# A two-layer graph and expert network on one core: record filling in small pieces, a last chunk 392 wide, and results added back by adding transfers

## The chip, the core and the metric

The kernel runs on one core of one Trainium2 chip. The core has five engines with queues of their own: TensorE (PE, matmuls into PSUM), VectorE (DVE), ScalarE (ACT), GpSimd (POOL) and SyncE (SP, here only a DMA queue). ScalarE and GpSimd issue DMAs too. All meet through semaphores: an instruction waits until a counter has reached a value. The metric is the device time in microseconds; lower is better. Before the change it was 1638.95 us, the median of 3 runs (1637.38 to 1642.18).

## What is computed

Inputs are 5000 rows of 128 features and a 5000 x 5000 adjacency of zeros and ones. Two layers follow each other, each a graph part and an expert part (mixture of eight experts, two per row):

```
x = x + gnn0(ln(x))  # A = adj * (y @ y.T); A / row_sum|A|; 0.9 * A @ ln(x) + 0.1 * h0
x = x + ffn0(ln(x))  # shared expert (hidden 512) + two of 8 private experts, weights from softmax
x = x + gnn1(ln(x))  # [x, adj @ x, sum_j adj[i,j] * adj[j,i]] @ weight + bias
x = x + ffn1(ln(x))  # two of 8 experts (hidden 256), erf-gelu
```

Everything is float32, the large products partly as a high and a low part of a shorter type (`F32R`, in the profile `fp32r`) that are multiplied separately and added.

## The kernel before

The 5000 rows are padded to 5120 = 10 column chunks of 512 (`CH`, `CW`) = 40 blocks of 128 (`NB`). `xres` holds the running x in SBUF, `xn` its norm. The kernel has four stages.

**First loop** (`a_iteration`, chunks k = 0 to 9, and two rounds more that drain). Chunk k has 43 steps s. In each of the first 40 steps PE makes a block `s` = y y^T, VectorE multiplies it with the adjacency block from `ring` into `m` (L1298), PE adds `xn` times `m` into the bank `agg` (L637), ScalarE takes |m| into `mabs` (L937), and PE adds groups of four `mabs` for the row sums (`d`, L681). `m` has four buffers, `mabs` eight. For some chunk pairs the outgoing adjacency is loaded too (`adj_out`); VectorE multiplies both (L1308), and PE sums the columns (`u`, L693). Beside this, at fixed steps (`A_AT`), chunk k-1 goes through the rest: division, residual, norm, router, and the scatter of its rows to DRAM by expert (`rows_scratch`, GpSimd, L1511), and chunk k-2 goes through the shared expert.

**Record filling.** Each expert's weights are gathered into one record in DRAM (`blob_scratch`), so that one DMA fetches them per tile. A record is: high and low part of the first weights, made by ScalarE (`whigh`) and VectorE (`wlow`) from `stage`, and the rest (second weights, biases), which goes from DRAM to DRAM. `store_rest` issues the rest on ScalarE's queue in step 6 of chunk 1, ten DMAs in a row. `wlow` has room for four experts, so `up_low(5)` must wait until the first half is stored (`low_written`).

**Expert tiles, layer 0** (`run_tiles(0, TILES)`): 27 tiles of 512 rows; the weighted results are scattered by GpSimd to `y_scratch` (L1520), two results per row in two halves (c = 0, 1).

**Second loop** (`z_iteration`). In pass k = 0, SyncE loads both halves of the results back chunk by chunk (`load_back`, L404) into `y_back`, VectorE adds them to `xres` (`back_add`, L1376), makes statistics, GpSimd the power -0.5 (L1497), VectorE the norm (L1041), ScalarE the high copy (L978), VectorE the low part. PE follows with the products of chunk column 0 (L768). Passes k = 1 to 9 (1 and 2 written out, 3 to 9 a hardware loop, `Fori`) split three of four adjacency blocks into high and low (ScalarE L989, VectorE L352) and multiply three times (L773 to L775). Beside this chunk k-1 goes through the graph weights, norm, router and row scatter, at the steps in `Z_AT`. `copy_aux`, `product`, `norm` (step 16), `weights` (33) and `scatter` (36) are such steps. The expert tiles of layer 1 and the output follow.

SyncE's queue is one list in order: all adjacency loads, the loads of the tiles, `load_back`, the loads of the second loop. Each engine's order is the order in which the code above is written out; nothing is reordered.

## Time and profile before

| | us |
|---|---|
| median of 3 runs (lowest, highest) | 1638.95 (1637.38, 1642.18) |
| profiled execution, its own time | 1639.02 |
| its span | 1637.2 |

| engine | busy us | share of the span |
|---|---|---|
| PE | 1397.8 | 85% |
| PEld (weight loads) | 864.9 | 53% |
| DVE | 967.8 | 59% |
| ACT | 646.0 | 39% |
| POOL | 541.9 | 33% |

The span is the time from the first to the last instruction in one profiled execution; 1.8 us of the device time lie outside it. Busy time overlaps between engines, so shares do not add up to one. The share of PE is a mean over stages: the first loop lasts to about 781 us, its drain to 830, the tiles of layer 0 to 1037, the second loop to 1461 (with its drain), the tiles of layer 1 to 1612, the rest is output. Line numbers (L637) are those of the kernel before. The letters in the rows below: `x8` is the number of instructions merged; in a timeline the bracket at the end says how long the engine had been idle and what ended it; `<-issue` is idle time that nothing in the profile explains.

### The profile page before, as it was taken

To read this page: it belongs to the slowest core of one execution; us is meant where nothing else is said; L and a number is where in the kernel's file an instruction comes from. 1 tells how busy PE (TensorE), PEld (TensorE's weight loads), DVE (VectorE), ACT (ScalarE), POOL (GpSimd) and SP (SyncE) were. 2 spreads that over 40 slices of the span, in tenths; PEclk is the share of its full clock that TensorE was granted. 3 is DMA by queue.
4 is the path that set the end of the run, shared out by engine and by line. 5 is a ranking of instruction groups with operands and counts; after the bars stand their busy time and mean duration, and the time that the engine had idled before them with its cause. 6 is when DMAs were issued, how large, how long until landed. Compare 5 with 4: busy or idle time off the path is not lost.

```text
span 1637.2 us, 22158 instructions
## 1 busy us (share of the span) xinstructions
PE 1397.8 (85%) x6742; PEld 864.9 (53%) x6742; DVE 967.8 (59%) x2697; ACT 646.0 (39%) x1067; POOL 541.9 (33%) x490
## 2 busy tenths in 40 slices
PE   5927699999999999999769999589999999838770
PEld 2413344444445454444558888346666666537660
DVE  7715475867676767676322322577777777633333
ACT  3504344434444434444224444135555555313330
POOL 1001101112020202112215555315555566537773
PEclk9968899999999999999779999799999999958995
DMA  9776788769696868785345554388888988436655
GB/s 324 266 224 209 284 303 311 284 245 326 252 339 229 331 226 322 250 309 201 148 156 189 180 192 156 114 309 297 306 296 302 311 294 312 142 91 184 183 164 195
DMA packets 105682, 399.29 MB, mean 244 GB/s; under 512 B 18800, under 2 KB 31123, under 8 KB 72819
## 3 DMA queue, kind: packets, MB, share of 16 engines
q1 hardware_dynamic: 63424, 337.25, 59.3%
q10 hardware_dynamic: 29330, 37.07, 6.8%
q0 software_dynamic: 12832, 23.81, 4.1%
q8 instruction: 47, 0.77, 0.2%
q14 instruction: 49, 0.39, 0.1%
HBM read 343.77 MB, written 59.51 MB: 246 GB/s over the span
## 4 chain that ended last, share of the span: by engine, by line
PE 56%; issue 12%; DVE 11%; POOL 8%; DMA 7%; ACTq 3%; ACT 2%; SPq 1%; DVEq 0%; POOLq 0%
PE agg L637 18%; PE s L621 6%; PE d L732 6%; PE d L681 5%; POOL y_scratch L1520 4%; POOL rows_scratch L1511 3%; PE d L577 3%; PE agg L768 2%; PE u L693 2%; DVE adj_over_wb L352 2%; PE u L717 2%; ACTq L848 2%; PE agg L773 1%; DMA rows_scratch<-xrow,idx 1%; PE u L719 1%
## 5 line engine op out<-in xcount | busy, mean ns | idle before, releaser
L637 PE MATMUL agg<-m,xn 128*128 128x512 f32 x800 | 411.1, 600 | 0.0
L1298 DVE TENSOR_TENSOR m<-s,ring 128x512 f32<-128x512 f32 x400 | 273.4, 687 | 226.6 <-PE s L621 144.9
L937 ACT ACTIVATE mabs<-m 128x512 f32<-128x512 f32 x400 | 247.6, 629 | 367.7 <-DVE m L1298 321.5
L621 PE MATMUL s<-ymov,ysta 128*128 128x512 f32 x400 | 258.8, 651 | 39.1 <-DVE m L1298 25.7
L1520 POOL DMA_INDIRECT y_scratch<-yo,ids x216 | 214.3, 992 | 168.5 <-DVE yo L1210 97.1
L1511 POOL DMA_INDIRECT rows_scratch<-xrow,idx x160 | 190.4, 1190 | 184.2 <-DVE idx L1141 98.8
L637 PEld LDWEIGHTS agg<-m,xn 128*128 128x128 f32 x800 | 153.9, 192 | 73.8 <-issue 53.0
L1497 POOL TENSOR_TENSOR rstd<-vareps,mhalf 128x4 f32<-128x4 f32 x30 | 35.0, 1167 | 455.1 <-DVE vareps L1035 455.1
L964 ACT ACTIVATE h<-u,wb 128x512 f32<-128x512 f32 x162 | 111.4, 688 | 173.0 <-PE u L719 172.5
L621 PEld LDWEIGHTS s<-ymov,ysta 128*128 128x128 f32 x400 | 76.4, 193 | 187.3 <-issue 102.7
L352 DVE TENSOR_TENSOR adj_over_wb<-ring,adj_over_wb 128x512 fp32r<-128x512 f32 x216 | 141.5, 686 | 47.4 <-ACT adj_over_wb L989 43.4
L732 PE MATMUL d<-wb,h 128*128 128x128 f32 x1296 | 164.7, 278 | 0.2 <-ACT h L964 0.2
L732 PEld LDWEIGHTS d<-wb,h 128*128 128x128 f32 x1296 | 160.1, 195 | 5.4 <-issue 0.6
L768 PE MATMUL agg<-ring,xn 128*128 128x512 f32 x260 | 131.7, 610 | 24.6 <-DVE xn L1041 24.6
L989 ACT CAST adj_over_wb<-ring 128x512 fp32r<-128x512 f32 x216 | 129.3, 620 | 54.6 <-PE agg L775 50.1
L681 PE MATMUL d<-mabs,ones 128*32 128x512 f32 x800 | 107.4, 609 | 39.1 <-ACT mabs L937 39.1
L1196 DVE TENSOR_TENSOR xnfl<-s,xnfh 128x512 fp32r<-128x512 f32 x54 | 37.2, 688 | 153.5 <-ACT xnfh L954 153.5
L773 PE MATMUL agg<-adj_over_wb,ysta 128*128 128x512 f32 x216 | 111.3, 515 | 14.5 <-DVE adj_over_wb L352 6.8
L717 PE MATMUL u<-xnfh,wb 128*128 128x512 f32 x162 | 76.1, 470 | 32.1 <-DVE xnfl L1196 27.1
L1559 POOL TENSOR_TENSOR ex<-euler,lg 128x8 f32<-128x8 f32 x40 | 74.5, 1887 | 59.9 <-DVE lg L1063 59.9
L1308 DVE CUSTOM_DVE_ANT_0 ring<-ring 128x512 f32<-128x512 f32 x132 | 89.7, 681 | 7.1 <-DMA ring<-in_adj_out 7.1
L775 PE MATMUL agg<-adj_over_wb,xnl 128*128 128x512 f32 x216 | 85.0, 394 | 0.0
(197 smaller groups left out, 1854.7 us busy)
## 6 DMA issues: line engine op xcount, KB each, us to landing
ring<-in_adj_in SPq DMA_DIRECT2D x200, 1024.0 KB, 5.8
ring<-in_adj_out SPq DMA_DIRECT2D x33, 1024.0 KB, 8.7
stage<-in_adj_out SPq DMA_DIRECT2D x22, 1024.0 KB, 8.8
wb<-blob_scratch SPq DMA_DIRECT2D x27, 834.0 KB, 4.5
rows_scratch<-yo ACTq DMA_DIRECT2D x81, 260.0 KB, 5.7
xt<-rows_scratch SPq DMA_DIRECT2D x54, 260.0 KB, 3.8
wb<-blob_scratch SPq DMA_DIRECT2D x27, 449.0 KB, 4.1
y_back<-y_scratch SPq DMA_DIRECT2D x10, 512.0 KB, 3.8
```

The lines of the kernel that those rows point to most:

```text
L352: return eng.tensor_tensor(low, raw, high.bitcast(F32), ALU.subtract)
L621: pe.matmul(sbank[s % 2][:], ysta[:, s * P:(s + 1) * P], ymov[:, k % 2, :], start=True, stop=True).then_inc(s_made, 1)
L637: pe.matmul(abank[:], xn[:, b, :], m[:, b % M_BUFS, :], start=b == 0, stop=b == NB - 1).then_inc(S["agg_blocks"], 1)
L681: last = pe.matmul(dbank[1][32 * i:32 * i + 32, :], ones[:, 0:32], mabs[:, (g * GROUPS + i) % ABS_BUFS, :], start=g == 0, stop=g == NB // ...
L732: last = pe.matmul(dbank[t % 2][:, q * D:(q + 1) * D], h[:, n % H_BUFS, q * P:(q + 1) * P], tile_part(t, "down", hb), start=hb == 0 and q ...
L768: pe.matmul(abank[:], xn[:, b, :], ring[:, l % 5, b % LB * CW:(b % LB + 1) * CW], start=b == 0, stop=b == NB - 1).then_inc(S["agg_blocks"], 1)
L773: pe.matmul(abank[:], xnh[:, b, :], hi, start=b == 0, stop=False)
L937: act.activation(mabs[:, b % ABS_BUFS, :], m[:, b % M_BUFS, :], ACT.Abs).then_inc(abs_made, 1)
L989: act.copy(adj_part(0, s), ring[:, l % 5, (s % LB) * CW:(s % LB + 1) * CW]).then_inc(adj_high, 1)
L1298: dve.tensor_tensor(m[:, s % M_BUFS, :], sbank[s % 2][:], slot_part(LOAD_AT[k, l, False][0], s % LB), ALU.mult).then_inc(m_made, 1)
L1511: pool.indirect_dma_start(out=rows_dram, out_offset=bass.IndirectOffsetOnAxis(ap=idx[:, t, c:c + 1], axis=0), in_=xrow[:, t, c, :], in_off ...
L1520: pool.indirect_dma_start(out=y_dram[layer], out_offset=bass.IndirectOffsetOnAxis(ap=ids[:, buf, q:q + 1], axis=0), in_=yo[:, buf, q, :], ...
```

## The change

It has three parts.

1. `store_rest` takes a piece number. A piece is one expert's slice (128 rows) or a row broadcast over all experts; there are 66 (`REST`), one in every fourth step from chunk 2 on. Of the low halves, VectorE makes only those of the shared expert and of experts 1 to 4 in chunk 1, the others in chunk 2, steps 4 to 7; the second low store moves from step 36 of chunk 1 to step 10 of chunk 2, the stores of layer 1 from step 24 to step 30, their splits from step 18 to step 22.
2. `width(k)` is 392 for the last chunk, else 512. In both loops loads, products, sums and splits of that chunk take 392 columns. For this the last pass of the second loop is written out, and the loop runs from 3 to 8. The semaphores `ring2_landed` are gone; `ring_landed` goes on counting.
3. `y_back`, `load_back` for layer 0 and `back_add` are gone. GpSimd issues twenty DMAs that add (`accum_op`) the two halves to `xres`, the second half of a chunk after the first has landed. The norm of pass 0 is made by ScalarE as `rstd * x + shift_n`, with `shift_n` from VectorE.

```
-                    if s == 6:
-                        act.wait_ge(b2_written, 32)
-                        act.wait_ge(small_landed, 16 * 7)
-                        store_rest(0)
-                        store_rest(1)
...
+                if agg and k > 1 and s % 4 == 0 and (k - 2) * NB // 4 + s // 4 < REST and s < NB:
+                    if k == 2 and s == 0:
+                        act.wait_ge(b2_written, 32)
+                        act.wait_ge(small_landed, 16 * 7)
+                    store_rest((k - 2) * NB // 4 + s // 4)
...
+        def store_rest(piece):
+            layer = 0 if piece < REST_OF[0] else 1
+            hid, piece = HID[layer], piece - layer * REST_OF[0]
+            e, i = divmod(piece, hid + 1)
+            if e == E:
+                row = b2_dram[1:1 + E, 0, :] if layer == 0 else b2_dram[0:E, 1, :]
+                act.dma_start(blob_dram[layer][:, :, 3 * hid * D:(3 * hid + 1) * D],
+                              row.unsqueeze(1).to_broadcast([E, P, D])).then_inc(rest_written, 16)
+            elif i == hid:
+                bias, first = ((b1, HID[0]), (b1z, 0))[layer]
+                act.dma_start(blob_dram[layer][e, :, (3 * hid + 1) * D:], bias[:, first + e * hid:first + (e + 1) * hid]).then_inc(rest_written, 16)
+            else:
+                act.dma_start(blob_dram[layer][e, :, (2 * hid + i) * D:(2 * hid + i + 1) * D],
+                              (w2p, w2_1)[layer][e, i * P:(i + 1) * P, :]).then_inc(rest_written, 16)
...
-                    if s == 36:
-                        store_low(0, 1)
...
-                        act.wait_ge(up_split, 1 + E)
+                        act.wait_ge(up_split, 1 + E // 2)
...
+                    if s == 10:
+                        store_low(0, 1)
...
-                if isinstance(k, int) and k == 1 and 24 <= s <= 24 + E:
+                if isinstance(k, int) and k == 1 and 24 <= s <= 24 + E // 2:
...
+                if isinstance(k, int) and k == 2 and 4 <= s < 4 + E // 2:
+                    up_low(1 + E // 2 + s - 4)
...
+def width(k):
+
+    return N - (CH - 1) * CW if isinstance(k, int) and k == CH - 1 else CW
...
-                    pe.matmul(abank[:], xn[:, b, :], m[:, b % M_BUFS, :], start=b == 0, stop=b == NB - 1
+                    pe.matmul(abank[:, 0:n], xn[:, b, :], m[:, b % M_BUFS, 0:n], start=b == 0, stop=b == NB - 1
...
-        with eng.Fori(3, CH) as k:
+        with eng.Fori(3, CH - 1) as k:
             iteration(k, True, True)
+        iteration(CH - 1, True, True)
...
-        for j in range(CH):
-            wait(sp, back_chain, 4 * (j - YIN_BUFS) + 2)
-            load_back(sp, y_back[:, j % YIN_BUFS], 0, j, yback_landed[j % YIN_BUFS])
...
+        def add_back(j, c):
+            pool.dma_start(xres[:, j * TB:(j + 1) * TB, :].rearrange("p t d -> p (t d)"),
+                           y_dram[0].rearrange("(c p b) d -> c p (b d)", c=2, p=P)[c, :, j * TB * D:(j + 1) * TB * D],
+                           accum_op=ALU.add).then_inc(yback_added[j % YIN_BUFS][c], 16)
+        def add_second(j):
+            pool.wait_ge(yback_added[j % YIN_BUFS][0], 16 * (j // YIN_BUFS + 1))
+            if j >= YIN_BUFS:
+                pool.wait_ge(yback_added[j % YIN_BUFS][1], 16 * (j // YIN_BUFS))
+            add_back(j, 1)
...
+        for j in range(YIN_BUFS):
+            add_back(j, 0)
+        for j in range(2):
+            add_second(j)
+            add_back(YIN_BUFS + j, 0)
...
                     power(s, back_var, back_rstd, s // TB + 1)
+                    if s // TB + 2 < CH:
+                        add_second(s // TB + 2)
+                    if s // TB + 2 + YIN_BUFS < CH:
+                        add_back(s // TB + 2 + YIN_BUFS, 0)
...
+            for b in range(c * TB, (c + 1) * TB):
+                last = act.activation(xn[:, b, :], xres[:, b, :], ACT.Identity, bias=shift_n[:, b:b + 1],
+                                      scale=rstd[:, b:b + 1])
```

ScalarE in chunk 1 of the first loop, before: after the copies of `b2rows` and four products the ten DMAs of the rest (`w2p`, `w_1` second weights, `b`, `b1z` biases, `b_scratch` rows) stand in a row.

```order
L864 DMA b_scratch<-b2rows 8x128
L937 ACTIVATE mabs<-m 128x512 x4
L848 DMA blob_scratch<-in_w2p 1024x1x128 x4
L851 DMA blob_scratch<-b 128x8x4
L854 DMA blob_scratch<-b_scratch 1024x1x128
L848 DMA blob_scratch<-in_w_1 1024x1x128 x2
L851 DMA blob_scratch<-b1z 128x8x2
L854 DMA blob_scratch<-b_scratch 1024x1x128
L822 DMA rows_scratch<-yo 128x520
```

The same place now, in which only the null rows (L840, before L822) stand between the products:

```order
L886 DMA b_scratch<-b2rows 8x128
L959 ACTIVATE mabs<-m 128x512 x4
L840 DMA rows_scratch<-yo 128x520
L959 ACTIVATE mabs<-m 128x512 x4
L840 DMA rows_scratch<-yo 128x520
```

The ten DMAs are gone from here; single ones, of 128 rows, now stand between products from chunk 2 on, as here in its steps 24 to 28:

```order
L876 DMA blob_scratch<-in_w2p 128x128
L959 ACTIVATE mabs<-m 128x512 x2
L840 DMA rows_scratch<-yo 128x520
L959 ACTIVATE mabs<-m 128x512 x2
L876 DMA blob_scratch<-in_w2p 128x128
```

GpSimd between the last result scatter of layer 0 and the second loop's router, before and now: the powers (`rstd`) of the ten chunks stood alone (the eleventh belongs to pass 1).

```order
L1520 DMA y_scratch<-yo,ids 10240x128 x108
L1497 TENSOR_TENSOR rstd<-vareps,mhalf 128x4 x11
L1559 TENSOR_TENSOR ex<-euler,lg 128x8 x4
```

```order
L1549 DMA y_scratch<-yo,ids 10240x128 x108
L1578 DMA xres<-y_scratch 128x512 x8
L1526 TENSOR_TENSOR rstd<-vareps,mhalf 128x4
L1578 DMA xres<-y_scratch 128x512 x2
L1526 TENSOR_TENSOR rstd<-vareps,mhalf 128x4
L1578 DMA xres<-y_scratch 128x512 x2
L1526 TENSOR_TENSOR rstd<-vareps,mhalf 128x4
```

Eight adding DMAs now come ahead of the first power, and two behind each of the next four. On VectorE the same stretch loses the adds and the norms and gets one small instruction a chunk; before:

```order
L1376 TENSOR_TENSOR xres<-xres,y_back 128x512 x2
L1024 BN_STATS stats<-xres 128x6 x4
L1032 BN_AGGR mv<-stats 128x2 x4
L1035 TENSOR_SCALAR vareps<-mv 128x4
L1041 TENSOR_SCALAR xn<-xres,mv,rstd 128x128 x4
L352 TENSOR_TENSOR xnl<-xn,ysta 128x512
```

and now:

```order
L1056 BN_STATS stats<-xres 128x6 x4
L1064 BN_AGGR mv<-stats 128x2 x4
L1067 TENSOR_SCALAR vareps<-mv 128x4
L1412 SCALAR_TENSOR_TENSOR shift_n<-mv,rstd 128x4
L361 TENSOR_TENSOR xnl<-xn,ysta 128x512
```

The two adds on `xres` and the four norms have left VectorE; the norms stand on ScalarE (`xn<-xres,shift_n,rstd`), ahead of its high copy.

## Rows read from the trace of the kernel before

**Rows 1.** windows of the first loop: chunk 1's stall, chunk 2, chunk 9.

```profile
core 0: us, PE busy (x) PEld busy (x) DVE busy (x) ACT busy (x) POOL busy (x), PEclk, DMA share, GB/s
77.00:128.00 51.00, 15.43 (x68) 7.29 (x67) 11.12 (x29) 5.32 (x11) 0.00 (x0) 0.70 0.74 231
190.00:270.00 80.00, 75.22 (x343) 36.24 (x342) 55.59 (x153) 34.21 (x56) 10.79 (x11) 0.98 0.87 314
...
708.00:781.00 73.00, 72.39 (x344) 35.43 (x340) 50.31 (x139) 30.21 (x51) 10.50 (x11) 1.00 0.61 221
```

**Rows 2.** waits of 78 to 190 us: us in all, times, longest.

```profile
PE d L681 <- ACT mabs L937: 36.1, 1, 36.1
...
PE s L621 <- DVE m L1298: 15.4, 3, 14.0
DVE wlow L352 <- DMA blob_scratch<-wlow: 15.1, 1, 15.1
```

**Rows 3.** timeline of ScalarE (start us, us): the `aggf` copies that open and end chunk 1.

```profile
77.15 0.59 ACT L916 COPY aggf<-agg 128x512 f32<-128x512 f32 x1 [1.22 <-PE agg L637]
...
191.94 0.59 ACT L916 COPY aggf<-agg 128x512 f32<-128x512 f32 x1 [1.22 <-PE agg L637]
```

**Rows 4.** two lines of DMA issues on ScalarE's queue, ns min/median/max.

```profile
L848 ACTq DMA_DIRECT2D blob_scratch<-in_w2p x4: 822/4411/8657, 85.5 to 100.2; - x4
...
L822 ACTq DMA_DIRECT2D rows_scratch<-yo x81: 338/338/3473, 22.0 to 769.1; - x81
```

**Rows 5.** waits of 190 to 270 us, chunk 2 of the first loop.

```profile
DVE ring L1308 <- DMA ring<-in_adj_out: 7.1, 2, 6.0
```

**Rows 6.** timeline of TensorE in chunk 9 of the first loop.

```profile
771.26 1.07 PE L681 MATMUL d<-mabs,ones 128*32 128x512 f32 x8
...
773.68 1.02 PE L637 MATMUL agg<-m,xn 128*128 128x512 f32 x2
...
774.77 1.02 PE L637 MATMUL agg<-m,xn 128*128 128x512 f32 x2
```

**Rows 7.** chain of waits in chunk 2: one group of eight column sums.

```profile
205.55 0.90 PE u L693 x8
```

**Rows 8.** groups of 708 to 781 us by shape: count, busy us, mean ns, idle before.

```profile
L1298 DVE TENSOR_TENSOR m<-s,ring 128x512 f32<-128x512 f32 x40 | 27.3, 688 | 22.0 <-PE s L621 16.5 <-issue 5.1 <-ACT mabs L937 0.3
```

**Rows 9.** timeline, start of the second loop: SyncE's queue, then PE, VectorE and GpSimd.

```profile
1039.33 27.12 SPq L404 DMA_DIRECT2D y_back<-y_scratch  x10
...
1050.67 1.22 PE L768 MATMUL agg<-ring,xn 128*128 128x512 f32 x1 [19.55 <-DVE xn L1041]
...
1058.32 1.11 DVE L1041 TENSOR_SCALAR xn<-xres,mv,rstd 128x128 f32<-128x128 f32 x4
...
1059.94 1.41 DVE L1376 TENSOR_TENSOR xres<-xres,y_back 128x512 f32<-128x512 f32 x2
...
1063.03 1.11 DVE L1041 TENSOR_SCALAR xn<-xres,mv,rstd 128x128 f32<-128x128 f32 x4
1063.20 1.03 POOL L1497 TENSOR_TENSOR rstd<-vareps,mhalf 128x4 f32<-128x4 f32 x1 [3.67 <-DVE vareps L1035]
...
1083.00 3.70 PE L768 MATMUL agg<-ring,xn 128*128 128x512 f32 x8 [1.00 <-DVE xn L1041]
```

**Rows 10.** the `aggf` copies of the second loop (ns, first and last start us).

```profile
L994 ACT COPY aggf<-agg x10: 586/586/586, 1094.9 to 1422.4; 128x512 f32<-128x512 f32 x10
```

**Rows 11.** DMA issues: KB each, us to landing; then the h0 load's issue.

```profile
y_back<-y_scratch SPq DMA_DIRECT2D x10, 512.0 KB, 3.8
...
L1534 POOL DMA_DIRECT2D aux<-in_h_t x10: 627/630/781, 26.8 to 734.3; - x10
...
DMA to landing us min/median/max: 4.4/7.1/8.7
```

**Rows 12.** timeline, last iteration of the second loop: norm of chunk 8, GpSimd's powers.

```profile
1400.97 1.11 DVE L1041 TENSOR_SCALAR xrow<-xres,mv,rstd 128x128 f32 x4 [1.34 <-DMA rows_scratch<-xrow,idx]
...
1406.49 7.59 POOL L1559 TENSOR_TENSOR ex<-euler,lg 128x8 f32<-128x8 f32 x4 [6.55 <-DVE lg L1063]
```

More of the change, by code:

```diff
@@ L48 @@
 FAR = 1e30
+REST_OF = tuple(E * (hid + 1) + 1 for hid in HID)
+REST = sum(REST_OF)
 BLOB = tuple(4 * D * hid - D * hid + D + hid for hid in HID)
@@ L91 @@
 LOAD_ORDER = load_order()
+SLOT_LOADS = [sum(ld[3] == slot for ld in LOAD_ORDER) for slot in range(5)]
 LOAD_AT = {(k, l, out): (slot, 16 * n) for k, l, out, slot, n, _ in LOAD_ORDER}
@@ L283, in bass_two_layer_gnn_moe_kernel @@
     ring_landed = [sem(f"ring_landed{i}") for i in range(7)]
-    ring2_landed = [sem(f"ring2_landed{i}") for i in range(5)]
     edges_read, redge_chain = sem("edges_read"), sem("redge_chain")
@@ L304, in bass_two_layer_gnn_moe_kernel @@
     y_scattered = [sem(f"y_scattered{i}") for i in range(YO_BUFS)]
-    yback_landed = [sem(f"yback_landed{i}") for i in range(YIN_BUFS)]
+    yback_added = [[sem(f"yback_added{i}_{c}") for c in range(2)] for i in range(YIN_BUFS)]
+    back_shift = sem("back_shift")
     back_chain, back_var, back_rstd = sem("back_chain"), sem("back_var"), sem("back_rstd")
@@ L356, in bass_two_layer_gnn_moe_kernel, with slot_part, slot_whole, adj_block @@
     Y_BLOCKS = YP // P
-    def slot_part(slot, b):
+    def slot_part(slot, b, n=CW):
         if slot < 5:
-            return ring[:, slot, b * CW:(b + 1) * CW]
-        return stage[:, ((slot - 5) * LB + b) * CW:((slot - 5) * LB + b + 1) * CW]
+            return ring[:, slot, b * CW:b * CW + n]
+        return stage[:, ((slot - 5) * LB + b) * CW:((slot - 5) * LB + b) * CW + n]
+    def slot_whole(slot, n):
+        whole = ring[:, slot, :] if slot < 5 else stage[:, (slot - 5) * LB * CW:(slot - 4) * LB * CW]
+        return whole if n == CW else whole.rearrange("p (b c) -> p b c", c=CW)[:, :, 0:n]
+    def adj_block(adj, k, l):
+        n, whole = width(k), adj[k, :, l * LB * CW:(l + 1) * LB * CW]
+        return whole if n == CW else whole.rearrange("p (b c) -> p b c", c=CW)[:, :, 0:n]
     def edges_done(k, l):
@@ L426, in load_adj @@
                 sp.wait_ge(up_split, 1 + E + 4)
-            adj, dst = (adj_out if out else adj_in), (ring[:, slot, :] if slot < 5 else
-                                                      stage[:, (slot - 5) * LB * CW:(slot - 4) * LB * CW])
-            sp.dma_start(dst, adj[k, :, l * LB * CW:(l + 1) * LB * CW]).then_inc(ring_landed[slot], 16)
+            sp.dma_start(slot_whole(slot, width(k)), adj_block(adj_out if out else adj_in, k, l)
+                         ).then_inc(ring_landed[slot], 16)
         def load_next(count):
@@ L612, in a_iteration @@
         def a_iteration(k, agg, mid, run_ffn):
-            S = SA
+            S, n = SA, width(k)
             for s in range(STEPS):
@@ L680, in add_abs @@
             for i in range(GROUPS):
-                last = pe.matmul(dbank[1][32 * i:32 * i + 32, :], ones[:, 0:32], mabs[:, (g * GROUPS + i) % ABS_BUFS, :],
+                last = pe.matmul(dbank[1][32 * i:32 * i + 32, 0:width(k)], ones[:, 0:32],
+                                 mabs[:, (g * GROUPS + i) % ABS_BUFS, 0:width(k)],
                                  start=g == 0, stop=g == NB // GROUPS - 1)
@@ L692, in add_cols @@
             for i in range(GROUPS):
-                last = pe.matmul(ubank[1][32 * i:32 * i + 32, :], ones[:, 0:32], slot_part(slot, i),
+                last = pe.matmul(ubank[1][32 * i:32 * i + 32, 0:width(k)], ones[:, 0:32], slot_part(slot, i, width(k)),
                                  start=l == columns[0], stop=l == columns[-1])
@@ L753, in z_iteration @@
         def z_iteration(k, agg, mid):
-            S = SZ
+            S, n = SZ, width(k)
             for s in range(STEPS):
@@ L988, in z_iteration @@
                         wait(act, SZ["agg_blocks"], (k - 1) * NB + split_block(i - ADJ_BUFS + SPLITS) + 1)
-                    act.copy(adj_part(0, s), ring[:, l % 5, (s % LB) * CW:(s % LB + 1) * CW]
-                             ).then_inc(adj_high, 1)
+                    act.copy(adj_part(0, s)[:, 0:width(k)], slot_part(l % 5, s % LB, width(k))).then_inc(adj_high, 1)
                 if mid and s == Z_AT["aggregate"]:
@@ L1306, in a_iteration @@
                         dve.wait_ge(ring_landed[outgoing], count)
-                    part = slot_part(outgoing, b % LB)
-                    dve.tensor_tensor_reduce(part, slot_part(into, b % LB), part, 1.0, 0.0, ALU.mult, ALU.add,
+                    part = slot_part(outgoing, b % LB, width(k))
+                    dve.tensor_tensor_reduce(part, slot_part(into, b % LB, width(k)), part, 1.0, 0.0, ALU.mult, ALU.add,
                                              rpart[:, k, b:b + 1]).then_inc(edges_read, 1)
```

97 lines of the change are left out of this document (45 added, 52 removed).

## The prediction

> **What bounds the kernel now.** I read the row of engines and the slices first. TensorE (PE) is busy 85% of the span, VectorE 59%, ScalarE 39%. So I look for the stretches where PE stands, and only then at the edits. The windows [rows 1] give these: in the first loop chunk 9 (708 to 781 us; the chunks from the fourth on are alike) takes 73 us with PE busy 72.4, but 77 to 128 us has PE busy 15.4 of 51. The waits of 78 to 190 us [rows 2] name the causes. ScalarE is late with `mabs`: PE stands 36.1 us at the group of row sums. Later VectorE stands 15.1 us before a split into `wlow`, because the store of the old `wlow` has not landed, and PE then waits 15.4 us in three waits. Chunk 1 thus lasts from 77.15 to 191.94, 114.8 us [rows 3]; without the two stalls it would be 63.3, fitting its smaller work.
>
> What holds ScalarE is its own queue: six issues of expert records, 0.82 to 8.66 us each [rows 4], two bias issues and two row issues follow each other in one place.
>
> **The change part by part.** All sums go against the profiled execution: span 1637.2, its own time 1639.02, 1.8 us outside the span; the median of the runs is 1638.95, so the two can be used alike.
>
> *1. Record filling in 66 pieces.* The ten issues leave chunk 1. The new pieces stand one in each fourth step from chunk 2 to chunk 8. A piece covers one expert, 128 descriptors where the old one had 1024. The nearest row of that size is the null-row store on the same queue, 128 rows, 0.338 us in the median [rows 4]; one eighth of the old 4.4 us is 0.55. Ten pieces a chunk are 3.4 to 5.5 us of ScalarE beside 30.2 busy in 73 [rows 1], and the products of `m` may run four blocks, 6 us, ahead of `mabs`, so this lies in cover. Two pieces (the row broadcasts) keep 1024 descriptors and are also shorter than those 6 us. Taken: 0 for the new pieces, -36.1 for the old wait. If the cover failed, the whole price of the pieces would be 66 x 0.55 = 36.
>
> *2. Second half of the low weights moved to chunk 2.* VectorE's splits 5 to 8 stand at steps 4 to 7 of chunk 2 and find the first store long landed (it is issued ten steps before the end of chunk 1). The wait disappears: -15.4 on PE. The next store, at step 10, must land before step 22: twelve steps of 1.9 us, 23 us, against a wait of 15.1 plus what came before it. Four splits more in chunk 2 (about 0.7 each, like the products, whose row comes below) go to VectorE, which has 24 us free in 80 [rows 1].
>
> *3. Traffic closer together.* Chunk 1's loads, a 2 MB weight load and 3 MB of stores now fall into some 63 us instead of 115; chunk 2, at a DMA share of 0.87 already [rows 1], gets 1 MB of store and ten pieces more. Against this, the last stores of chunk 2 move from step 24 to step 30, behind the last of its seven outgoing loads. Before, one of these loads came late and VectorE waited 6.0 us [rows 5]. I take that gain and the return of as much in late loads: 0, bounds -6 (wait gone, nothing returns) and +12 (both chunks get such a wait twice).
>
> *4. Last chunk 392 wide in the first loop.* A step of PE in chunk 9 takes 1.09 us (start to start of the `agg` pairs), a group of eight `d` 1.07 [rows 6], a group of column sums 0.90 [rows 7]. So 40 x 1.09 + 10 x 1.07 + 5 x 0.90 = 58.8 us of the 73 are proportional to the width; 120 of 512 columns is 23.4%, 13.8 us. VectorE's product costs 27.3 us in 40 [rows 8] and falls less, as part of each instruction is fixed; in blocks that also read the outgoing adjacency it comes level with PE. I take -12; bounds -8 (VectorE bounds the 20 paired blocks) and -14.
>
> *5. Layer 0 results added by transfers.* Before, the loads start at 1039.33 and the first `agg` of the second loop at 1050.67. Per chunk VectorE needs 4.71 us (norm at 1058.32, next at 1063.03), of which two adds 1.41 and four norms 1.11; PE's eight matmuls need 3.70 and stand 1.00 [rows 9]. The first pass ends at 1094.9 [rows 10], 55.5 us after the loads start. Now the adds (GpSimd queue) and norms (ScalarE) leave VectorE, which drops to about 2.4 us a chunk. PE would be next with 3.6, if the new chain lets it: two adding transfers after each other, statistics (4.71 - 1.41 - 1.11 less the split, about 1.75), the power on GpSimd (1.03 [rows 9]), the shift, four ScalarE norms (about 1.2, an estimate from half of a 128x512 copy's 0.59 each [rows 3] and below; bounds 0.6 and 2.4). The second add of chunk c+2 is issued behind the power of chunk c, so two chunks take one L + 3.6 (L: issue to landing of one adding transfer; 1.03 + 1.75 and the semaphores). End of the pass: 2L + 5.1 for the first chunk, 4 x (L + 3.6) for the pairs, 2 x 3.6 for the last two on PE: 6L + 26.7 us. It equals the old 55.5 at L = 4.8. The trace has no adding transfer. The nearest is the h0 load, same size, shape and queue: 4.4 to 8.7 us, median 7.1, issue 0.63 [rows 11]; that median fell in a DMA share of 0.6 to 0.9. A plain load of twice the size lands here in 3.8 us [rows 11]. As the second loop's loads are fewer here, I take 5.3, nearer the lower end of h0: 58.5, so +3. Bounds: L = 3.8 gives 49.5 (-6), L = 8.7 gives 78.9 (+23).
>
> The trace speaks for a fixed landing time of 4.4 us or more on this queue. The Trainium skill (DMA: Bandwidth & Descriptors, Anatomy of one DMA — SWDGE (gpsimd) path) gives 2.0 us plus the bytes over 436 GB/s, which would be 2.6 us for 256 KB. This case's h0 rows disagree, 4.4 at the least. By that page of the Trainium skill the pass would be bound by PE (11 + 36 us) and this term -8; it says nothing of the add itself.
>
> *6. Last chunk of the second loop.* An iteration takes (1422.4 - 1094.9) / 9 = 36.4 us [rows 10]. All of it scaled would give 8.5. But two things in iteration 9 do not scale: the norm of chunk 8 starts at 1400.97 only because the row scatter of chunk 7 has landed, and GpSimd's four powers run from 1406.49 to 1414.08 [rows 12]. VectorE's weights (step 33) wait for these. So the last seven blocks start no earlier than about 1415.2 and take 0.7 each: 1420, gain 2.4. I take -2.5; bounds 0 and -8.5. That this iteration is written out instead of looped costs nothing I can see.
>
> Sum: -36.1 - 15.4 + 0 - 12 + 3 - 2.5 = -63. Time 1639.0 - 63 = 1576.
>
> **The rivals.**
> *A: the adding transfers are slow.* For it: h0's median of 7.1 and that an add reads its destination too. Against: fewer loads in the way. L = 7.1 to 8.7 gives +14 to +23 instead of +3: 1587 to 1596.
> *B: the stall comes back as late loads.* For it: chunk 2 at share 0.87 with a wait of 6.0, and three stores at the end of chunk 1. Against: two to three loads lie ahead of their use, and the old filling's own traffic leaves chunk 1. Half of the 51.5 would return less the 6: +20, 1596.
> *C: the first pass of the second loop becomes PE's.* L below 3.8: term 5 is -6 to -8, term 3 is -6: 1559 to 1562. The rule of the Trainium skill above would bring this about.
> *D: slower than before.* An issue may cost per instruction, not per descriptor. Then each of the ten pieces of a chunk holds ScalarE for t, and a chunk takes 33 + 10t (30.2 busy, null-row issues) as soon as that is above 73. Seven chunks must lose 68 (the 63 and 5 more to be told): t above 5.0 us. At 8.66, the longest issue seen, it is 7 x 46.6 = +326: 1902. Against: the first of the old issues took 0.82, and 128-row stores 0.34 [rows 4]; the long ones look like a full queue, which spaced pieces do not fill.
> *E: the change does not do what it says.* The pieces wait somewhere else: the expert tiles wait for all 66, but the last is issued in the middle of chunk 8, more than a whole chunk before the first tile. I see no place.
>
> **How the numbers follow.** Main case (1562 to 1587) 0.68; A 0.11; B 0.10; C 0.09; D 0.015; E 0.005, no change. The main case's time is 1576. The range must leave out at most 2 in 10: from C's 1560 to B's 1598 leaves D, the far ends of A and B together, and more of C. The main case alone runs from 1562 to 1587. About 0.3% (5 us) is what a measurement can tell from no change. Faster by more: 0.97; within: 0.01; slower: 0.02.
>
> **What would show it.** Right: no ScalarE queue row above 2 us in 80 to 130 us except the row broadcasts, chunk 1 near 61 to 67 us from one `aggf` copy to the next; in chunk 9 of the first loop `agg` pairs 0.84 us apart and 61 us in all; the new issues near 0.35 to 0.55 us; VectorE's adds gone from the start of the second loop, with its first pass ending 53 to 61 us after the last scatter; the last iteration near 34 us with the norm waiting for the row scatter. Wrong: VectorE waits of several us for `ring` in chunks 1 and 2 (B), landings above 7 us on the adding transfers (A), `mabs` late in chunks 2 to 8 (D), or the last iteration of the second loop near 28 us, which would mean that the row scatter does not pin it.

## The result, and the profile after

| | before | after |
|---|---|---|
| time, median (lowest to highest), us | 1638.16 (1634.82 to 1642.18), 4 runs | 1579.70 (1577.78 to 1592.07), 4 runs |
| span of the profiled execution, us | 1637.2 | 1576.0 |
| ratio of the times | | 0.9657, 95% interval 0.9619 to 0.9695 |

Faster by 58.5 us; 1576 was forecast. The page of after, busy us of the engines:

```profile
PE 1377.3 (87%) x6742; PEld 863.4 (55%) x6742; DVE 934.2 (59%) x2647; ACT 654.7 (42%) x1107; POOL 559.6 (36%) x510
```

Between the two profiled executions lie 61.2 us. The `aggf` copies that close each chunk cut both spans at the same places (stage lengths, us):

| stage | before | after | difference |
|---|---|---|---|
| chunk 1, first loop | 114.8 | 61.3 | -53.4 |
| chunk 2 | 79.3 | 82.5 | +3.2 |
| chunks 3 to 8 | 436.7 | 438.6 | +1.9 |
| chunk 9 (392 wide) | 73.0 | 60.1 | -12.9 |
| end of first loop to first load or adding transfer | 258.4 | 255.9 | -2.5 |
| from there to the end of the first pass | 55.6 | 64.4 | +8.8 |
| passes 2 to 9 of the second loop | 290.5 | 291.2 | +0.7 |
| its last pass | 37.0 | 31.6 | -5.4 |
| tail | 214.8 | 213.0 | -1.8 |

The rest (0.2) lies ahead of chunk 1. These are lengths in two single executions; where two kernels of the first chip run the same code they still differ, by 5 us in chunk 2 (81.5 to 86.4 in after and experiments 5 to 7) and by 1 to 3 elsewhere. Windows of after, which answer to [rows 1] (us, busy time of each engine with its instructions, granted clock, DMA share, GB/s):

```profile
77.00:128.00 51.00, 49.66 (x206) 22.50 (x206) 37.51 (x102) 25.77 (x46) 7.49 (x8) 1.00 0.86 318
140.00:220.00 80.00, 72.88 (x330) 34.77 (x329) 57.24 (x155) 32.44 (x54) 10.78 (x11) 0.98 0.92 341
660.00:720.00 60.00, 59.46 (x344) 35.00 (x340) 42.22 (x139) 25.91 (x51) 10.49 (x11) 1.00 0.65 211
```

In the stretch where TensorE had worked 15 of 51 us it now works 49.7. Chunk 2 moves 341 GB/s where it had moved 314. Over all of chunk 1, before and then after:

```profile
77.15:191.94 114.79, 63.33 (x246) 27.76 (x249) 45.43 (x114) 32.05 (x56) 10.52 (x11) 0.79 0.74 244
```

```profile
77.35:138.70 61.35, 60.02 (x246) 26.51 (x249) 42.85 (x110) 31.91 (x56) 10.48 (x11) 1.00 0.89 328
```

The same 246 matmuls keep TensorE busy 3.3 us less. Before, its granted clock was 0.50 (1.2 GHz) from 100 to 130 us, while it stood, and 0.79 on average; in after it was 1.00 (2.4 GHz) throughout. The timeline of ScalarE puts chunk 1 between the first two of these copies and chunk 2 between the last two, against 114.8 us for chunk 1 in [rows 3]:

```profile
77.35 0.59 ACT L938 COPY aggf<-agg 128x512 f32<-128x512 f32 x1 [1.22 <-PE agg L654]
...
138.70 0.59 ACT L938 COPY aggf<-agg 128x512 f32<-128x512 f32 x1 [1.22 <-PE agg L654]
...
221.20 0.59 ACT L938 COPY aggf<-agg 128x512 f32<-128x512 f32 x1 [1.22 <-PE agg L654]
```

The waits of 140 to 225 us of after (us in all, times, longest) show what became of the second stall of [rows 2] and of the late load of [rows 5]:

```profile
ACT mabs L959 <- issue: 14.0, 3, 7.6
...
DVE wlow L361 <- DMA blob_scratch<-wlow: 5.7, 1, 5.7
PE s L638 <- DVE m L1332: 4.7, 5, 1.4
...
PE d L698 <- ACT mabs L959: 2.9, 1, 2.9
...
DVE ring L1342 <- DMA ring<-in_adj_out: 2.2, 3, 1.7
```

VectorE still waits for the first low store, 5.7 us instead of 15.1. New is ScalarE's 14.0 us with the cause "issue". Its queue's own timeline in chunk 2 says where:

```profile
142.72 5.62 ACTq L876 DMA_DIRECT2D blob_scratch<-in_w2p  x1
...
198.49 0.39 ACTq L851 DMA_DIRECT2D blob_scratch<-whigh  x1
198.92 0.84 ACTq L859 DMA_DIRECT2D blob_scratch<-wlow  x1
199.79 6.83 ACTq L840 DMA_DIRECT2D rows_scratch<-yo  x1
206.73 2.63 ACTq L876 DMA_DIRECT2D blob_scratch<-in_w2p  x1
209.50 3.66 ACTq L840 DMA_DIRECT2D rows_scratch<-yo  x1
```

The null-row store, 0.34 us in the median, takes 6.83 right behind two large stores. I read this, and the old pieces [rows 4], as an issue that waits for room in its queue; no row shows the room itself. Most pieces are short. All of one line (ns min/median/max, first and last start):

```profile
L876 ACTq DMA_DIRECT2D blob_scratch<-in_w2p x32: 518/518/5622, 136.9 to 424.2; - x32
L876 ACTq DMA_DIRECT2D blob_scratch<-in_w x16: 518/518/562, 446.6 to 611.0; - x16
```

Chunk 9 on TensorE, answering to [rows 6]: the `agg` pairs now start 0.84 us apart (1.09 before), eight `d` take 0.87 (1.07 before).

```profile
712.28 0.87 PE L698 MATMUL d<-mabs,ones 128*32 128x392 f32 x8
...
713.36 0.82 PE L654 MATMUL agg<-m,xn 128*128 128x392 f32 x2
...
714.20 0.82 PE L654 MATMUL agg<-m,xn 128*128 128x392 f32 x2
```

The adding transfers, by their line (issue on GpSimd in ns, who waits, landing):

```profile
L1578 POOL DMA_DIRECT2D xres<-y_scratch x20: 864/1059/1949, 975.8 to 1023.4; - x20
...
  DVE stats L1056: 39.9, 10
...
DMA to landing us min/median/max: 3.8/7.0/12.7
```

And the start of the second loop, which answers to [rows 9], in its timeline:

```profile
975.77 3.70 POOL L1578 DMA_DIRECT2D xres<-y_scratch  x4 [1.68 <-issue]
980.37 1.76 POOL L1578 DMA_DIRECT2D xres<-y_scratch  x2 [0.90 <-DMA xres<-y_scratch]
983.87 1.77 POOL L1578 DMA_DIRECT2D xres<-y_scratch  x2 [1.75 <-DMA xres<-y_scratch]
987.55 0.87 DVE L1056 BATCH_NORM_STATS2 stats<-xres 128x6 f32<-128x128 f32 x4 [19.06 <-DMA xres<-y_scratch]
...
991.94 1.65 ACT L999 ACTIVATE xn<-xres,shift_n,rstd 128x128 f32<-128x128 f32 x4 [26.86 <-DVE shift_n L1412]
...
993.64 16.30 PE L786 MATMUL agg<-ring,xn 128*128 128x512 f32 x32 [26.61 <-ACT xn L999]
```

The first chunk is complete 11.8 us after the first issue, and TensorE starts 17.9 us after it (before: 11.3 us after the first load). From there to the end of the pass TensorE is busy 39.1 us in both kernels. What it waits beside that in after are two stretches, and they come after SyncE has begun to load adjacency again:

```profile
999.67 40.95 SPq L525 DMA_DIRECT2D ring<-in_adj_in  x10
...
1013.34 3.70 PE L786 MATMUL agg<-ring,xn 128*128 128x512 f32 x8 [3.40 <-ACT xn L999]
...
1020.99 19.13 PE L786 MATMUL agg<-ring,xn 128*128 128x512 f32 x40 [3.95 <-ACT xn L999]
```

So of the 8.8 us some 6.5 are the later start and 2.2 are waits (7.4 us against 5.1 before). Since no load runs beside the adding transfers up to 999.67, windows show what they cost the DMA engines (after first, then before, same columns):

```profile
981.00:990.00 9.00, 0.00 (x0) 0.00 (x0) 1.42 (x9) 0.00 (x0) 3.65 (x5) 0.50 1.02 173
```

```profile
1044.00:1050.00 6.00, 0.00 (x0) 0.00 (x0) 5.25 (x24) 0.00 (x0) 1.74 (x2) 0.50 0.78 275
```

Adding, the engines are busy throughout and move 173 GB/s; plain loads of the same data had moved 275 at a share of 0.78 (they were issued by SyncE; experiment 6 keeps GpSimd's queue).

In the last pass the norm and GpSimd's powers of [rows 12] stand at:

```profile
1344.38 1.12 DVE L1073 TENSOR_SCALAR xrow<-xres,mv,rstd 128x128 f32<-128x128 f32 x4 [0.57 <-POOL rstd L1526]
```

```profile
1349.54 7.19 POOL L1614 TENSOR_TENSOR ex<-euler,lg 128x8 f32<-128x8 f32 x4 [5.31 <-DVE lg L1095]
```

The norm starts 13.0 us into the pass (15.6 before), and no DMA holds it. The whole last pass, before and then after:

```profile
1385.36:1422.36 37.00, 34.91 (x150) 23.90 (x150) 27.55 (x80) 18.75 (x33) 20.84 (x15) 1.00 0.58 201
```

```profile
1331.36:1362.96 31.60, 29.05 (x150) 22.78 (x150) 24.03 (x80) 15.74 (x33) 18.43 (x13) 1.00 0.58 180
```

TensorE is busy for all but 2.1 and 2.6 us of it.

### The profile page after: what moved, and what is told of

The parts are those of the page before. It is cut to its first block and busy times, and to the rows that moved or that the text cites. A ratio compares the mean times of both kernels' runs of the same rounds, so it can differ in the third digit from the quotient of the medians.

```text
span 1576.0 us, 22128 instructions
## 1 busy us (share of the span) xinstructions
PE 1377.3 (87%) x6742; PEld 863.4 (55%) x6742; DVE 934.2 (59%) x2647; ACT 654.7 (42%) x1107; POOL 559.6 (36%) x510
## 5 line engine op out<-in xcount | busy, mean ns | idle before, releaser
L654 PE MATMUL agg<-m,xn 128*128 128x512 f32 (+1 forms) x800 | 400.7, 587 | 0.0
L1332 DVE TENSOR_TENSOR m<-s,ring 128x512 f32<-128x512 f32 (+1 forms) x400 | 268.2, 675 | 188.2 <-PE s L638 140.9
L959 ACT ACTIVATE mabs<-m 128x512 f32<-128x512 f32 (+1 forms) x400 | 243.1, 619 | 314.4 <-DVE m L1332 297.1
L638 PE MATMUL s<-ymov,ysta 128*128 128x512 f32 (+1 forms) x400 | 252.3, 635 | 24.8 <-DMA ymov<-ysta 13.3
L361 DVE TENSOR_TENSOR adj_over_wb<-ring,adj_over_wb 128x512 fp32r<-128x512 f32 (+1 forms) x216 | 138.4, 671 | 49.2 <-ACT adj_over_wb L1022 45.4
L786 PE MATMUL agg<-ring,xn 128*128 128x512 f32 (+1 forms) x260 | 129.7, 605 | 34.0 <-ACT xn L999 34.0
L1022 ACT CAST adj_over_wb<-ring 128x512 fp32r<-128x512 f32 (+1 forms) x216 | 126.7, 608 | 54.4 <-PE agg L793 50.0
L791 PE MATMUL agg<-adj_over_wb,ysta 128*128 128x512 f32 (+1 forms) x216 | 109.1, 505 | 15.7 <-DVE adj_over_wb L361 8.4
L698 PE MATMUL d<-mabs,ones 128*32 128x512 f32 (+1 forms) x800 | 105.7, 601 | 5.9 <-ACT mabs L959 5.9
L1342 DVE CUSTOM_DVE_ANT_0 ring<-ring 128x512 f32<-128x512 f32 (+1 forms) x132 | 88.2, 670 | 2.2 <-DMA ring<-in_adj_out 2.2
```

Of the source, the lines that this page charges most:

```text
L361: return eng.tensor_tensor(low, raw, high.bitcast(F32), ALU.subtract)
L638: pe.matmul(sbank[s % 2][:, 0:n], ysta[:, s * P:(s + 1) * P], ymov[:, k % 2, 0:n], start=True, stop=True).then_inc(s_made, 1)
L654: pe.matmul(abank[:, 0:n], xn[:, b, :], m[:, b % M_BUFS, 0:n], start=b == 0, stop=b == NB - 1).then_inc(S["agg_blocks"], 1)
L786: pe.matmul(abank[:, 0:n], xn[:, b, :], slot_part(l % 5, b % LB, n), start=b == 0, stop=b == NB - 1).then_inc(S["agg_blocks"], 1)
L791: pe.matmul(abank[:, 0:n], xnh[:, b, :], hi, start=b == 0, stop=False)
L959: act.activation(mabs[:, b % ABS_BUFS, 0:width(k)], m[:, b % M_BUFS, 0:width(k)], ACT.Abs).then_inc(abs_made, 1)
```

## The experiments

Experiments 1 to 4 ran on a second chip (before: 1706.86 us there) and 9 to 11 on a third (1691.85), so compare ratios and stage lengths within a chip. Numbers 5 to 8 ran where before takes 1643.08, near the 1638.16 of the first comparison. The changed kernel itself did not run on the second chip; experiments 1 to 4 are set against each other there, stage by stage. Each of 6, 7 and 8 is a single run, read by its stages and not by its time: the four runs of the changed kernel span 14 us.

**1. The ten old issues back at step 6 of chunk 1.**

```
-                if agg and k > 1 and s % 4 == 0 and (k - 2) * NB // 4 + s // 4 < REST and s < NB:
...
+                    if s == 6:
+                        act.wait_ge(b2_written, 32)
+                        act.wait_ge(small_landed, 16 * 7)
+                        store_rest_all(0)
+                        store_rest_all(1)
```

> The changed kernel with the ten record DMAs back in step 6 of chunk 1 in a row; everything else as changed. Theory (the parts add up; the stall is ScalarE's queue, 36 us of PE idle in the old trace): chunk 1 of the first loop, 61.4 us after the change, becomes 96 to 99 us, chunk 2 loses the queue holds of the first piece (5.6 us) and falls from 82.5 to about 79; time 1579.7 + 36 - 3 = 1613. Rival (what chunk 1 had really lacked was DMA bandwidth, so part of the 36 us was cover for the weight load and the stores): chunk 1 becomes only 85 to 90 us, time about 1603.

1683.09 us, ratio 0.9875 (0.9835 to 0.9914); chunk 1 took 100.4 us, chunk 2 79.5. The waits of 78 to 185 us:

```profile
ACT mabs L971 <- issue: 45.6, 2, 41.5
...
PE d L698 <- ACT mabs L971: 34.8, 1, 34.8
```

Chunk 1 is 38 us longer than in experiments 3 and 4 (62.4 and 62.5), chunk 2 4 to 5 us shorter (84.6 and 83.1). The first term stands: this part alone is the stall of 35 us. Chunk 1 came out 1.4 us above the theory's range, and the rival (85 to 90) is refuted.

This is also the only kernel on this chip with no piece in chunks 3 to 8. They took 442.5 us here and 449.5 to 456.2 in experiments 2 to 4. Of these 7 to 14 us TensorE's own busy time is 5 to 10 (at a granted clock of 0.98 to 0.99 against 1.00), and 2 to 4 are idle. On the first chip the same chunks took 436.7 us without pieces and 437.0 to 438.6 with them (three kernels; 440.2 in experiment 7). Whether the pieces cost something on the second chip is open, as one profile of each kernel is all there is.

**2. The second half of the low weights back in chunk 1.**

```
+                    if s == 36:
+                        store_low(0, 1)
...
-                if isinstance(k, int) and k == 2 and 4 <= s < 4 + E // 2:
-                    up_low(1 + E // 2 + s - 4)
```

> The changed kernel with all eight low splits and both low stores back in chunk 1; the 66 pieces stay spread. Theory: VectorE waits some 15 us for the first low store again, chunk 1 becomes 75 to 77 us; chunk 2 loses the store at step 10 and the 5.7 us wait for the low store before step 22 and falls from 82.5 to about 77; time 1579.7 + 15 - 5 = 1589. Rival (prediction's term by itself, nothing comes back in chunk 2): +15, 1595.

1662.13 us, ratio 0.9738 (0.9695 to 0.9780); chunk 1 took 78.3 us, chunk 2 80.1. The waits of 78 to 170 us:

```profile
PE s L638 <- DVE m L1330: 16.2, 4, 14.2
DVE wlow L361 <- DMA blob_scratch<-wlow: 15.3, 1, 15.3
```

The second term stands: chunk 1 is 16 us longer than in experiments 3 and 4. Of this, 3.0 to 4.5 us are given back in chunk 2 (83.1 and 84.6 us in experiments 4 and 3, which have the splits there). Both chunks came out above the theory (75 to 77, and 77).

**3. The last chunk 512 wide in both loops.**

```
-    return N - (CH - 1) * CW if isinstance(k, int) and k == CH - 1 else CW
+    return CW
```

> The changed kernel with the last chunk 512 wide in both loops again (the last pass of the second loop stays written out). Theory from the two traces: chunk 9 of the first loop from 60.1 back to 73.0, last pass of the second loop from 31.6 to 36.5: +17.8, 1597.5. The prediction's own terms (12 and 2.5) would give +14.5, 1594. Rival (the written-out pass is itself a gain): the second loop's last pass stays below 35.5 us at full width.

1661.08 us, ratio 0.9748 (0.9694 to 0.9803). Chunk 9 took 73.8 us and the last pass 36.3; in the other kernels of this chip they took 62.1 to 63.7 and 31.6 to 32.2. Written out at full width the last pass is as long as a looped one (36.0 to 37.1), so I read the width as the whole gain; it is 4.1 to 4.7 us here, and the first comparison's 5.4 starts from a pass of 37.0.

**4. The adding transfers undone, adds and norms on VectorE.**

```
+        for j in range(CH):
+            wait(sp, back_chain, 4 * (j - YIN_BUFS) + 2)
+            load_back(sp, y_back[:, j % YIN_BUFS], 0, j, yback_landed[j % YIN_BUFS])
...
-        for j in range(YIN_BUFS):
-            add_back(j, 0)
...
-                    back_norm(s // TB)
+            norm_apply(c * TB, lambda t: xres[:, c * TB + t, :], lambda t: xn[:, c * TB + t, :], back_rstd, c + 1, back_made)
```

> The changed kernel with the layer 0 results loaded by SyncE into a buffer and added by VectorE, norm on VectorE, as before the change; no adding transfer. Theory (the adding transfers land in 7.0 us in the median and pace the first pass of the second loop, 64.4 us against 55.6): the pass returns to 55 to 56 us, time 1579.7 - 9 = 1571. Rival (the prediction's +3 was right for the part and the rest of the 9 us is scatter of the stage before): -3, 1577.

1644.56 us, ratio 0.9646 (0.9582 to 0.9711). From the end of the first loop to that of the first pass it took 324.3 us against 334.6 to 335.7 in experiments 1 to 3; the pass itself took 55.5 us from its first load, as in before. By this stage the third part of the change is a loss of 10 to 11 us, 8.4 to 9.1 of them in the pass itself. The ratio does not show it: it cannot be told from the changed kernel's 0.9657, where the theory had 0.959. Chunks 3 to 8, in which the two run the same code, were the longest of this chip here (456.2 us).

**5. The same, but the norms stay on ScalarE.** Against the changed kernel:

```
-            dve.wait_ge(yback_added[c % YIN_BUFS][1], 16 * (c // YIN_BUFS + 1))
+            dve.wait_ge(yback_landed[c % YIN_BUFS], 16 * (c // YIN_BUFS + 1))
...
+                dve.tensor_tensor(xs, xs, y_back[:, c % YIN_BUFS, i, :].rearrange("p (t d) -> p t d", t=TB), ALU.add
...
```

> The changed kernel with the results loaded by SyncE and added by VectorE as before the change, but the norm left on ScalarE. Theory (PE's 3.7 us a chunk and VectorE's adds are then about level, no adding transfer in the way): VectorE needs 4.71 - 1.11 + 0.15 = 3.8 us a chunk, the first pass of the second loop takes about 12 + 10 x 3.8 + 2 = 52 us instead of 64.4; ratio to the kernel before 0.9657 - 12/1638 = 0.958. Rival (ScalarE's four norms at 1.65 us and the longer chain of four engines eat it): the pass stays at 55 to 56 us, ratio 0.960.

1563.86 us (1561.16 to 1577.48), ratio 0.9542 (0.9484 to 0.9599). The pass took 49.0 us from its first load (64.4 with adding transfers). TensorE's whole pass in the timeline:

```profile
987.71 36.85 PE L793 MATMUL agg<-ring,xn 128*128 128x512 f32 x80 [20.29 <-ACT xn L1006]
```

Eighty matmuls in one run: TensorE is the bound from its first instruction. The pass is shorter than the theory's 52. This version beats both kernels, and its interval lies clear of the changed kernel's.

**6. The transfers of the changed kernel without the add.**

```
-                           accum_op=ALU.add).then_inc(yback_added...
+                           ).then_inc(yback_added...
```

> The changed kernel with the twenty adding transfers replaced by plain copies of the same size, queue, order and waits (leaves the addition out: xres is overwritten by the results). Theory (the add itself occupies the DMA engines: in the changed kernel's trace they are fully busy at 173 GB/s before any other load runs, plain loads reach 257 to 275 at a share of 0.78): landing falls from a median of 7.0 to 4 to 5 us, the pass from 64.4 to about 54. Rival (it is GpSimd's queue and the traffic around it, as the h0 loads' median of 7.1 suggested): landing stays at 6 to 7 us, the pass at 62 to 65.

One run: 1564.17 us. The halves overwrite `xres` instead of being added; all else is as in after. The line's issue and landing:

```profile
L1578 POOL DMA_DIRECT2D xres<-y_scratch x20: 541/572/597, 971.5 to 1010.1; - x20
...
DMA to landing us min/median/max: 2.9/4.0/7.2
```

The pass took 54.4 us, as the theory had it: same queue, same order, 10 us less. TensorE started 12.6 us after the first issue instead of 17.9. It is the add that costs, in issue (0.57 instead of 1.06 us) and in landing (4.0 instead of 7.0). The last six plain transfers, beside the adjacency loads, landed in 5.1 to 7.2 us, the eight at the start in 2.9 to 4.8: other traffic costs too.

**7. The second loop's first loads held back until the adding is nearly done.**

```
+        for i in range(YIN_BUFS):
+            sp.wait_ge(yback_added[i][1], 16 * (3 if i < 2 else 2))
```

> The changed kernel with the adjacency loads of blocks 20 and on held back until the last adding transfer has landed, so that these run alone. Theory of the occupied engines: landing stays high, 4.5 to 6 us in the median, as several adds are in flight at 170 GB/s, but the 12.7 us outliers go, and the last add lands by about 40 us after the first is issued. Rival (only the loads beside them make them late): landing 3.8 to 4.5 us throughout. The pass itself gets longer in both, as PE then waits for the held loads.

One run: 1588.04 us. From the end of the first loop to that of the pass it took 324.5 us against 320.3 (TensorE waits 12.6 us for the held loads); another 3.9 us lie in chunk 2, where nothing was edited. Alone, the adding transfers still land in 5.8 us (median), and the window in which only they run reads:

```profile
986.00:996.00 10.00, 0.00 (x0) 0.00 (x0) 1.42 (x9) 0.00 (x0) 3.85 (x5) 0.50 1.04 179
```

179 GB/s at a share of 1.04. The median hides what the other loads do. The three transfers that the changed kernel issues 26.0 to 29.0 us after the first one, beside the adjacency loads, landed there in 8.1, 11.3 and 12.7 us; the same three landed here in 4.5, 6.0 and 5.0. The first eight, which run alone in both, land in 4.3 to 8.7 and 4.3 to 8.2 us. So the late start is the add's own price, and the two later waits of TensorE come from adding with the loads beside it. The theory held in its median and its outliers (8.2 at most); the last add landed 45.5 us after the first issue, not 40.

**8. Ten large pieces as in before, spaced over chunks 3 to 7.**

```
+                if agg and 3 <= k <= 7 and s in (8, 28):
...
+                    store_big((k - 3) * 2 + (s == 28))
```

> The changed kernel with the ten record DMAs in their old size (1024 descriptors), but one every half chunk from chunk 3 to chunk 7 (steps 8 and 28) instead of 66 small ones. Theory (the long issues of the old kernel were a full queue): each issues in 0.8 to 2 us, and no PE wait on mabs appears: chunks 3 to 7 stay within 1 us of the changed kernel's 72 to 75. Rival (the issue costs per descriptor, 4.4 us for 1024): ScalarE is held 4 to 5 us at each, at the edge of the four-block cover, and the chunks get 1 to 3 us longer.

One run: 1580.95 us. Six of the ten issues:

```profile
L884 ACTq DMA_DIRECT2D blob_scratch<-in_w2p x4: 709/718/828, 232.3 to 342.8; - x4
L884 ACTq DMA_DIRECT2D blob_scratch<-in_w x2: 711/712/714, 456.8 to 491.5; - x2
```

An issue of 1024 rows takes 0.71 us spaced and 4.4 (median) in a row [rows 4]; one of 128 rows takes 0.52. Cutting the pieces small was not needed, spacing them was. Chunks 3 to 7 took 72.1 to 74.8 us; two of them are 1.6 above the changed kernel's, which is outside the theory's 1 us, but experiment 7, with the small pieces, has the same (74.9 and 74.3). TensorE nowhere waited for `mabs` in them. Chunk 2, without any piece in it, still took 81.7 us, and with the pieces it took 81.5 to 86.4 on this chip, so here its length does not come from them. (On the second chip 79.5 without pieces, in experiment 1, stands against 83.1 and 84.6 with them, which would allow a part.)

**9. Number 5 with chunk 2 eased.**

```
-                        store_low(1, 0)
-                if agg and k > 1 and s % 4 == 0 and (k - 2) * NB // 4 + s // 4 < REST and s < NB:
+                if agg and k > 2 and s % 4 == 0 and (k - 3) * NB // 4 + s // 4 < REST and s < NB:
...
+                if isinstance(k, int) and k == 3 and s == 10:
+                    store_low(1, 0)
```

> The changed kernel with the results of layer 0 loaded back on SyncE and added by VectorE (the norms stay on ScalarE), and with chunk 2 of the first loop eased: no record piece in chunk 2 (pieces from chunk 3 on), the last four low-weight splits and the store of the high weights four steps later, and the store of the first half of layer 1's low weights in chunk 3 instead of chunk 2. Theory: chunk 2 is long (82.5 us against 72 to 75) because its stores and loads share the DMA engines and VectorE waits 5.7 us for the low weights' store to land; with one store less and the wait shorter, chunk 2 falls to 75 to 79 us and chunk 3 stays under 76: 3 to 6 us under the version with VectorE's adds alone, ratio to before 0.949 to 0.952. Rival (what is moved out of chunk 2 comes back in chunk 3, the engines being full in both): the sum of chunks 2 and 3 stays at 156 to 158 and the ratio at 0.954.

**10. The changed kernel again,** with no edit.

> The changed kernel as it is, beside the two others on one chip. Expected: ratio 0.966 as in its first measurement, chunk 2 at 82 us, the first pass of the second loop ending 64 us after its first adding transfer is issued.

**11. Number 5 again,** with the edit shown there.

> The changed kernel with only the adding transfers replaced (results of layer 0 loaded back on SyncE, added by VectorE, norms on ScalarE), a second time and on the same chip as the changed kernel. Expected: 14 to 18 us under the changed kernel, ratio to before 0.955; if the first result came from the chip, the two are alike.

| | us | ratio to before | chunk 2 | chunk 3 | first loop's end to first pass's end |
|---|---|---|---|---|---|
| 9 | 1614.83 (1606.66 to 1618.62) | 0.9554 (0.9523 to 0.9585) | 78.3 | 74.9 | 311.0 |
| 10 | 1637.49 (1632.86 to 1643.20) | 0.9686 (0.9655 to 0.9717) | 84.9 | 74.9 | 334.4 |
| 11 | 1613.39 (1611.55 to 1617.99) | 0.9548 (0.9518 to 0.9579) | 81.5 | 73.2 | 316.5 |

Number 10 repeats the first comparison (0.9686 where 0.966 was expected; the pass took 65.0 us). Numbers 10 and 11 repeat the gain of experiment 5: 24 us on this chip, more than the 14 to 18 expected, 17.9 of them in the stage of the adding (the rest lies mostly in the first loop and ahead of it, where the two run the same code). In number 9 the null-row store stands behind one large store instead of two, and its issue is short again:

```profile
199.96 0.39 ACTq L858 DMA_DIRECT2D blob_scratch<-whigh  x1
200.38 0.60 ACTq L847 DMA_DIRECT2D rows_scratch<-yo  x1
```

Chunk 2 is 3.2 us shorter and chunk 3 1.7 longer than in number 11, and the two times cannot be told apart. Each chunk lies where the theory had it (75 to 79, under 76), but the 3 to 6 us in all do not show: the two together took 153.2 us against 154.7. The rival's 156 to 158 for the sum is not met either. The long issue is gone with the second large store ahead of it, but easing it gained nothing that this measurement tells.

## Why the prediction was right, and where it was off

- **Record filling (-36.1).** Right, cause and size: experiment 1 brings back a wait of 34.8, chunk 1 38 us longer and chunk 2 4 to 5 shorter. On the first chip chunks 3 to 8 rose by 1.9 us at most with the pieces (experiment 7: 3.5); the second chip leaves this open. Experiment 8 shows that it was not the size of the old pieces that made their issues long but their standing in a row; a full queue is the reading that fits. Rival D falls with the pieces' median issue of 0.52 us.
- **Low weights (-15.4).** Right in the sum, wrong in one step. I wrote that the moved splits "find the first store long landed". The 5.7 us wait above is that store: it is issued at 122.66 us, lands 27.5 us later, and VectorE's wait for it ends at 150.28, in chunk 2. Where VectorE stood for it, it landed in half the time: 14.5 us in before and 14.7 in experiment 2; now the first loop runs on beside it, and the DMA engines carry 382 GB/s instead of 345. The step that failed is the landing time, which I took from a stretch in which the engines stood. Chunk 1 gained 53.4 instead of 51.5, because the granted clock did not fall in it (3.3 us, above), and chunk 2 paid.
- **Closer traffic (0, bounds -6 to +12).** Chunk 2 rose by 3.2 us and the chunks behind it by 1.9. The late load of 6.0 [rows 5] did shrink to 2.2 in three waits, as I took. What returned was not a late load (rival B) but waits for stores: VectorE's 5.7 us above, and ScalarE's own issue behind two stores, which TensorE waits 2.9 us for. That wait is the sign that I had named for rival D, from another cause. That the two stores of layer 1 stand together at step 30 is a detail that I had read only as a gain.
- **Chunk 9 (-12).** -12.9; scaling with the width held, and experiment 3 takes 10 to 12 of it back on the second chip.
- **Adding transfers (+3, bounds -6 to +23).** The direction was right, the size was not: +8.8 (8.4 to 9.1 by experiment 4). The term that was mis-sized is L = 5.3, taken near the low end of h0 because fewer loads run here; it measured 7.0 in the median, which is rival A's landing. The h0 median of 7.1 [rows 11] would have been the better row. The reason I gave failed in both ways: without any other load the first eight adding transfers took 4.3 to 8.7 us (experiment 6, without the add, 2.9 to 4.8), and the adjacency loads of the second loop did run beside the later ones, up to 12.7 us. The formula 6L + 26.7 was wrong too. With L = 7.0 it gives 68.7 us where the pass took 64.4, with experiment 6's 4.0 it gives 50.7 where that took 54.4: the pass does not pay L once per two chunks, TensorE starts late and then waits twice. So rival A's landing did not bring its +14. Two things under it were not in the sum: an issue on GpSimd takes 1.06 us (0.63 for h0), and the first chunk completes after 11.8 us. The norms took 1.65 us, where I had put 1.2. Rival C, a pass bound by TensorE, did not come with adding transfers; experiment 5 made one with plain loads, 49.0 us. By the Trainium skill (DMA: Bandwidth & Descriptors, Anatomy of one DMA — SWDGE (gpsimd) path) a transfer of 256 KB takes 2.6 us, an estimate from its figures. The plain transfers of experiment 6 come nearest, with 2.9 at the least and 4.0 in the median; the adding ones, 3.8 and 7.0, do not follow it.
- **Last pass (-2.5, bounds 0 to -8.5).** -5.4. The step that failed: "starts at 1400.97 only because the row scatter of chunk 7 has landed". In after that norm waits for GpSimd's power 0.57 us and starts 2.6 us earlier; the wait shown in [rows 12] was the last to end, not a fixed time. What follows the powers scaled as well: 8.3 us from their end to the pass's in before, 6.2 in after. And the path through norm and powers was hardly what set the pass in the first place: TensorE was busy 34.9 of 37.0 us and is now busy 29.1 of 31.6, and that 5.9 us of its own work explains the 5.4.
- **Not forecast.** -2.5 us before the first adding transfer, and -1.8 in the tail. The tail is chance as far as the runs tell: with the same code it took 212.6 to 215.0 us in the kernels of the first chip, and 214.8 in before. The other stage took 254.6 to 255.9 there against 258.4 in before; its cause is open.

The span fell by 61.2 us where I had 63. So good a total is partly luck: gains beyond the forecast in chunk 1 (1.9), chunk 9 (0.9), the last pass (2.9) and the two places not forecast (4.3) stand against 5.1 lost in chunks 2 to 8, 5.8 in the first pass and 0.9 elsewhere.

## What to carry to other kernels

Space the stores that an engine issues between its own work: right behind large ones even a short issue became a stall of several us here (0.34 to 6.83), and the engine that issues it pays. A landing time that was read while the engines stood does not carry over to a stretch in which they run (14.5 and 27.5 us for the same store). An adding transfer takes work off VectorE, but in this kernel it cost more in issue, landing and DMA time than it saved; where TensorE waits for the data, try a plain load and an add on VectorE with the norm on another engine first. When a wait is the last of several to end, moving it shows the next one, so do not treat its end as a fixed time.
